# Linear attention: half of the next batch's scores move ahead of the second half's values

## The chip, the cores and the metric

The kernel runs on one core of a Trainium2 chip. The metric is the device time of one execution in microseconds (us), the median over several runs. Engines: TensorE (PE, its weight loads apart as PEld), VectorE (DVE), ScalarE (ACT), GpSimd (POOL) and SyncE (SP, which only starts transfers here).

## The reference, cut to what matters

The program is six layers over x of shape (8, 512, 128), each added to x: a mixture of experts, linear attention, the same experts again, a gated MLP with 4-bit rounding, softmax attention, and the MLP again. The change is in the linear attention:

```
qkv = (x @ qkv_w.T)                      # x normalised; 16 heads of 8
phi_q = relu(q) + EPS ; phi_k = relu(k) + EPS
kv = einsum('bhnd,bhne->bhnde', phi_k, v)
S = cumsum(kv, axis=2)                   # over the tokens n
out = einsum('bhnd,bhnde->bhne', phi_q, S)
out = out / max(scale * pos, EPS)
x = x + out @ proj_w.T
```

## The kernel before

All eight batches of x stay in SBUF. In this stage one body handles one batch i of 512 tokens, as 4 tiles of 128 tokens, each cut into 4 chunks of 32 tokens (c), and the 16 heads as 4 groups of 4 heads (g). The causal sum is split in two parts that add up in PSUM:

- within a chunk: `scores` multiplies keys by queries of the same 32 tokens, by head; VectorE masks them with the causal triangle (`scores` in its block, line 962) into `probs`; `within` multiplies the values by them.
- across chunks: `states` makes the key-value product of each chunk, ScalarE copies it out (`take_states`, line 547), GpSimd sums them up along the tokens (`linatt_prefix`, line 355), and `across` multiplies the summed states by the queries, onto the banks of `within`.

`within` and `across` are done in two halves, chunks 0 and 1, then chunks 2 and 3. Both halves use PSUM banks 6 and 7, so between them VectorE must take the result out. That is `pick`, the choice of heads: of four columns sets it keeps in each row the one of its own head, in three steps into `picked` (each counted on the semaphore `pick_part`), and a last one, in two parts, into `attT` (counted on `attT_ready`). The scores of one batch take 32 matmuls for each pair of groups; the pair 0 goes to banks 2 and 3, the pair 1 to banks 4 and 5. The matmuls appear as two records each in the trace.

The order on TensorE in body(i) is written by hand and looks ahead by one batch: input projection of batch i+1 (keys to bank 1, queries to bank 0, values to bank 2), turning of the keys (bank 3), `within` half 0 of batch i, `states` of i+1 (banks 2 to 5), `across` half 0, output projection of batch i-1 (bank 1), transposes of batch i+2 (bank 0), `within` half 1, `across` half 1, and all `scores` of batch i+1. The input projection waits until the output projection's result in bank 1 has been added to x (`residual`), which it knows from a signal of VectorE's later work: it waits for `attT_ready` of the whole `pick` of half 1.

VectorE in body(i): four masks of batch i, the keys of i+1 between the second and third, queries of i+1, statistics of a later batch, `pick` half 0, `residual` of batch i-1, `pick` half 1. ScalarE: queries, values and keys of batch i+1 out of PSUM, four copies of the queries with all heads but one zeroed (`q_bd`, line 539), four copies of the states, and the normalised rows of a later batch. Body 0, a loop of two passes with two bodies each (1 to 4), and bodies 5, 6 and 7 make up the stage. Body 7 has no next batch; its VectorE also begins the rounding of weights for a later layer.

Each engine runs its own list in order, and semaphores hold them together; `pe.wait_ge(s[...], n)` holds everything behind it on TensorE.

Of the kernel before, what the change touches and what calls it, by code (L numbers as in the profile page):

```python
# [24 lines left out]
P = 128  # L25
B, T, C = 8, 512, 128
TPB = T // P
# [4 lines left out]
CH = 32  # L32
NCH = P // CH
HQ = CH // HD
# [41 lines left out]
def macaron(nc, x, qkv_w, proj_w, alpha_log, beta_log, router_w, w1, w2,  # L76
            in_w, in_b, out_w, out_b, w_gate, w_up, w_down, out):
    with ExitStack() as ctx:
# [651 lines left out]
        def _(dve):  # L730
# [213 lines left out]
            def linatt(s, nxt):  # L944
                ch = Chain(dve, s["dve_chain"])

                def keys(i):

                    dve.wait_ge(s["k_done"], i + 1)
                    nc.vector.tensor_scalar(phi_k[:, :], bank(1, T), 0.0, ATT_EPS, ALU.max, ALU.add).then_inc(s["phik_ready"], 1)  # L950

                def queries(i):

                    dve.wait_ge(s["reluq_ready"], i + 1)
                    if type(i) is int and i == 0:
                        prep.settle()
                    nc.vector.scalar_tensor_tensor(phi_q[:, :], relu_q, ATT_EPS, pos[:, :],
                                                   ALU.add, ALU.mult).then_inc(s["phiq_ready"], 1)

                def scores(i, g, side):  # L960
                    dve.wait_ge(s["score_done"], 2 * i + g // 2 + 1)
                    nc.vector.tensor_tensor(probs[:, side, g, :, :, :].rearrange("p j h n -> p (j h) n"),
                                            bank(2 + g, TPB * HQ, CH),
                                            causal[:, :].unsqueeze(1).to_broadcast([P, TPB * HQ, CH]),
                                            ALU.mult).then_inc(s["probs_ready"], 1)

                def pick(i, half, side):

                    dve.wait_ge(s["att_done"], 2 * i + half + 1)
                    both = ps[:, 6:8, :].rearrange("p c (j h n) -> p (c j) h n", j=TPB, h=HQ)  # L970
                    nc.vector.tensor_scalar(picked[:, :, :], both[:, :, 0, :], headsel[:, 0:1], None,
                                            ALU.mult).then_inc(s["pick_part"], 1)
                    for hh in range(1, HQ - 1):

                        dve.wait_ge(s["pick_part"], 6 * i + 3 * half + hh)
                        nc.vector.scalar_tensor_tensor(picked[:, :, :], both[:, :, hh, :], headsel[:, hh:hh + 1],  # L976
                                                       picked[:, :, :], ALU.mult, ALU.add).then_inc(s["pick_part"], 1)

                    dve.wait_ge(s["pick_part"], 6 * i + 3 * half + 3)
                    for a in range(2):  # L980
                        c = 2 * half + a
                        t = nc.vector.scalar_tensor_tensor(attT[:, side, :, CH * c:CH * c + CH],
                                                           bank(6 + a, TPB, HQ * CH)[:, :, CH * (HQ - 1):CH * HQ],
                                                           headsel[:, HQ - 1:HQ], picked[:, TPB * a:TPB * a + TPB, :],
                                                           ALU.mult, ALU.add)
                    t.then_inc(s["attT_ready"], 1)

                def residual(i):
                    dve.wait_ge(s["proj_done"], i + 1)
                    nc.vector.tensor_tensor(group_b(i), bank(1, TPB, C), group_b(i), ALU.add).then_inc(s["x_done"], 1)  # L990

                def body(i, side):
                    more = known_below(i, GROUPS - 1)
                    scores(i, 0, side)
                    scores(i, 1, side)
                    if more:
                        keys(i + 1)
                    scores(i, 2, side)
                    scores(i, 3, side)
                    if more:  # L1000
                        queries(i + 1)
                    if known_below(i, GROUPS - 3):
                        ch.start(i * PER["linatt"] + pre)

                        dve.wait_ge(s["xn_ready"], i + 3)
                        ln_stats(s, ch, i + 3, TPB, tile_b)
                        assert ch.k == PER["linatt"], ("linatt", ch.k)
                    elif i == GROUPS - 3:
                        ch.start(i * PER["linatt"] + pre)
                        dve.wait_ge(s["xn_ready"], GROUPS)  # L1010
                        ln_stats(nxt, ch, 0, TPB, tile_b)
                    if not more:

                        dve.wait_ge(s_fw, 80)
                        w4.largest()
                        w4.scales()
                        w4.inverse()
                    pick(i, 0, side)
                    if not (type(i) is int and i == 0):
                        residual(i - 1)  # L1020
                    if not more:
                        w4.divide()
                    pick(i, 1, side)

                keys(0)
                queries(0)
                dve.wait_ge(s["xn_ready"], 2)
                ln_stats(s, ch, 2, TPB, tile_b)
                pre = ch.k
                linatt_bodies(dve, body)  # L1030
                dve.wait_ge(nxt["xn_ready"], 1)
                ln_stats(nxt, ch, 1, TPB, tile_b)
                residual(GROUPS - 1)
                dve.wait_ge(s["x_done"], GROUPS)
# [186 lines left out]
        def _(pe):  # L1221
# [98 lines left out]
            def linatt(s, nxt):  # L1320
                def project_in(i):
                    pe.wait_ge(s["xnT_ready"], i + 1)
                    if type(i) is not int or i > 1:

                        pe.wait_ge(s["attT_ready"], 2 * (i - 1))
                    mm(bank(1, T), wqkvT[:, 1, :], xnT[:, 0:T]).then_inc(s["k_done"], 1)
                    mm(bank(0, T), wqkvT[:, 0, :], xnT[:, 0:T]).then_inc(s["q_done"], 1)
                    if type(i) is not int or i > 0:

                        pe.wait_ge(s["probs_ready"], HQ * (i - 1) + 1)  # L1330
                    for j in range(TPB):
                        t = mm(bank(2, TPB, C)[:, j, :], tok(j), wqkvT[:, 2, :])
                    t.then_inc(s["v_done"], 1)
# [22 lines left out]
                                   tile_position=(CH * c, 0))  # L1356
                    t.then_inc(s["state_done"], 1)

                def scores(i, side):

                    pe.wait_ge(s["qbd_ready"], HQ * i + HQ)

                    pe.wait_ge(s["state_taken"], HQ * i + HQ)
                    pe.sem_inc(s_passed_pe, 1)
                    for pair in range(HQ // 2):
                        for j in range(TPB):
                            for c in range(NCH):
                                cols = slice(P * j + CH * c, P * j + CH * c + CH)
                                for g in (2 * pair, 2 * pair + 1):
                                    r = slice(CH * g, CH * g + CH)  # L1370
                                    t = mm(bank(2 + g, TPB, P)[CH * c:CH * c + CH, j, :], phi_k[r, cols],
                                           q_bd[r, side, :, cols], tile_position=(CH * g, CH * c))
                        t.then_inc(s["score_done"], 1)

                def within(i, half, side):

# [41 lines left out]
                def body(i, side):  # L1418
                    more = known_below(i, GROUPS - 1)
                    if more:  # L1420
                        project_in(i + 1)
                        turn_keys(i + 1)
                    within(i, 0, side)
                    if more:
                        states(i + 1, 1 - side)
                    across(i, 0, side)
                    if not (type(i) is int and i == 0):
                        project_out(i - 1, 1 - side, more)
                    if more:

                        pe.wait_ge(s["reluq_ready"], i + 2)
                        if known_below(i, GROUPS - 2):
                            transposes(s, i + 2)
                        else:
                            transposes(nxt, 0)
                    within(i, 1, side)
                    across(i, 1, side)
                    if more:
                        scores(i + 1, 1 - side)

                pe.wait_ge(s_wT, 2)
                project_in(0)
# [1 line left out]
                states(0, 0)  # L1444
                pe.wait_ge(s["reluq_ready"], 1)
                transposes(s, 1)
                scores(0, 0)
                linatt_bodies(pe, body)
                project_out(GROUPS - 1, 1, False)

# [200 lines left out]
```

## Time and profile before

| | |
|---|---|
| median of 3 runs | 820.65 us (819.05 to 822.27) |
| profiled execution | 819.17 us, its span 817.5 us |
| TensorE busy | 682.5 us, 83% of the span; mean granted clock 0.932 |
| VectorE, ScalarE, GpSimd busy | 77%, 58%, 29% |
| DMA | 7.00 MB, mean 9 GB/s |

The span runs from the first to the last instruction. The granted clock is TensorE's, as a share of full speed (2.4 GHz). Times in timelines are us from the start of the span. A few per cent of matmul records can be missing.

### The profile page before, as it was taken

To read this page: it belongs to the slowest core of one execution; us is meant where nothing else is said; L and a number is where in the kernel's file an instruction comes from. 1 tells how busy PE (TensorE), PEld (TensorE's weight loads), DVE (VectorE), ACT (ScalarE), POOL (GpSimd) and SP (SyncE) were. 2 spreads that over 40 slices of the span, in tenths; PEclk is the share of its full clock that TensorE was granted. 3 is DMA by queue.
4 is the path that set the end of the run, shared out by engine and by line. 5 is a ranking of instruction groups with operands and counts; after the bars stand their busy time and mean duration, and the time that the engine had idled before them with its cause. 6 is when DMAs were issued, how large, how long until landed. Compare 5 with 4: busy or idle time off the path is not lost.

```text
span 817.5 us, 16964 instructions
## 1 busy us (share of the span) xinstructions
PE 682.5 (83%) x5826; PEld 492.9 (60%) x5826; DVE 632.0 (77%) x1594; ACT 473.4 (58%) x915; POOL 239.5 (29%) x375
## 2 busy tenths in 40 slices
PE   5999999789988799999957788838898873787885
PEld 3777767577777667777734465534645652455654
DVE  2887888456655668878969999846999975899993
ACT  3877786664663078777755566526454214575652
POOL 5011020456455000110013543011643442345400
PEclk9999999699999699999978999978999995899997
DMA  8000000000000000000000000000000000000000
GB/s 210 2 0 0 0 1 1 2 3 4 0 1 4 2 1 0 0 0 1 0 1 0 1 0 0 0 0 2 1 0 0 0 1 0 1 26 13 23 16 26
DMA packets 13454, 7.00 MB, mean 9 GB/s; under 512 B 1176, under 2 KB 13408, under 8 KB 13408
## 3 DMA queue, kind: packets, MB, share of 16 engines
q1 hardware_dynamic: 11328, 5.33, 2.5%
q10 hardware_dynamic: 2080, 1.05, 0.5%
q8 instruction: 29, 0.48, 0.2%
q14 instruction: 17, 0.14, 0.1%
HBM read 4.28 MB, written 2.10 MB: 8 GB/s over the span
## 4 chain that ended last, share of the span: by engine, by line
PE 45%; DVE 36%; issue 10%; ACT 5%; POOL 2%; DVEq 1%; DMA 0%; ACTq 0%; POOLq 0%
PE ps L1250 41%; DVE ffn_work L786 4%; DVE shared L1046 3%; DVE shared L1074 3%; DVE x_sb L888 3%; DVE fq_h_max L753 2%; DVE ffn_work L1162 2%; DVE ffn_work L791 2%; DVE hq L797 2%; DVE picked L976 2%; DVE stats L822 2%; PE ps L1572 2%; ACT ffn_work L440 2%; ACT xn L470 2%; DVE ffn_work L780 1%
## 5 line engine op out<-in xcount | busy, mean ns | idle before, releaser
L1250 PEld LDWEIGHTS ps<-w_sb,sq_h 128*128 128x128 f32 x1024 | 131.4, 191 | 70.2 <-ACT sq_h L492 51.7
L888 DVE SCALAR_TENSOR_TENSOR x_sb<-ps,gates,x_sb 128x128 f32 (+1 forms) x512 | 147.1, 343 | 22.5 <-PE ps L1250 18.7
L1250 PE MATMUL ps<-w_sb,sq_h 128*128 128x128 f32 x1024 | 137.7, 277 | 1.5 <-ACT sq_h L492 1.4
L1250 PE MATMUL ps<-xnT,w_sb 128*128 128x512 f32 x256 | 135.2, 612 | 0.0
L310 POOL TENSOR_SCALAR vareps<-meanvar 128x4 f32<-128x4 f32 (+1 forms) x44 | 22.5, 511 | 354.3 <-DVE meanvar L831 338.3
L488 ACT ACTIVATE relu_h<-ps 128x512 f32<-128x512 f32 x128 | 75.7, 592 | 59.5 <-PE ps L1250 59.2
L470 ACT ACTIVATE xn<-x_sb,shift,rstd 128x128 f32 (+1 forms) x192 | 79.7, 481 | 17.6 <-POOL shift L318 17.6
L492 ACT ACTIVATE sq_h<-relu_h 128x512 f32<-128x512 f32 x128 | 80.6, 630 | 4.1
L676 ACT ACTIVATE hqT<-ps 128x384 f32<-128x384 f32 x64 | 30.0, 489 | 67.4 <-PE ps L1572 66.5
L1250 PE MATMUL ps<-gateT,xnT 128*128 128x352 f32 x128 | 56.8, 528 | 14.2 <-ACT ffn_work L670 10.7
L1250 PE MATMUL ps<-downT,hqT 128*128 128x128 f32 x384 | 62.7, 306 | 3.2 <-ACT hqT L676 3.0
L1572 PE MATMUL ps<-ident,hq 128*128 128x128 f32 x192 | 35.2, 313 | 34.9 <-DVE hq L797 34.9
L1250 PEld LDWEIGHTS ps<-downT,hqT 128*128 128x128 f32 x384 | 54.9, 215 | 9.3 <-ACT hqT L676 8.9
L355 POOL TENSOR_TENSOR shared<-shared 128x128 f32<-128x128 f32 x112 | 50.9, 455 | 28.9 <-ACT shared L547 20.8
L822 DVE BATCH_NORM_STATS2 stats<-x_sb 128x6 f32 (+1 forms) x192 | 40.7, 276 | 23.2 <-ACT xn L470 7.9
L1572 PEld LDWEIGHTS ps<-ident,hq 128*128 128x128 f32 x192 | 26.0, 161 | 48.0 <-DVE hq L797 48.0
L363 POOL TENSOR_TENSOR shared<-shared 128x512 f32<-128x512 f32 x32 | 42.8, 1365 | 39.3 <-DVE shared L1074 39.3
L440 ACT ACTIVATE ffn_work<-ffn_work 128x512 f32<-128x512 f32 (+2 forms) x33 | 33.5, 1015 | 34.2 <-DVE ffn_work L780 34.2
L1250 PE MATMUL ps<-upT,xnT 128*128 128x352 f32 x128 | 52.9, 498 | 0.0
L315 POOL TENSOR_TENSOR rstd<-vareps,minus_half 128x4 f32<-128x4 f32 (+1 forms) x44 | 51.3, 1166 | 3.7
L786 DVE SCALAR_TENSOR_TENSOR ffn_work<-ffn_work 128x512 f32<-128x512 f32 (+2 forms) x33 | 38.4, 1162 | 12.3 <-ACT ffn_work L440 12.2
L1046 DVE TENSOR_TENSOR shared<-shared 128x1024 f32<-128x1024 f32 x32 | 41.0, 1349 | 5.8 <-ACT shared L588 5.8
(156 smaller groups left out, 1265.5 us busy)
## 6 DMA issues: line engine op xcount, KB each, us to landing
x_sb<-in_L_attn_x_dram SPq DMA_DIRECT2D x8, 256.0 KB, 6.9
out_dram<-x_sb SPq DMA_DIRECT2D x8, 256.0 KB, 2.3
w_sb<-in_L_ffn_w_all_dram ACTq DMA_DIRECT2D x2, 512.0 KB, 6.1
wraw<-in_L_attn_qkv_w_dram SPq DMA_DIRECT2D x1, 192.0 KB, 4.9
wraw<-attn_in_proj_weight_dram SPq DMA_DIRECT2D x1, 192.0 KB, 4.1
fraw<-in_L_ffn_w_down_dram SPq DMA_DIRECT2D x1, 176.0 KB, 2.8
fraw<-in_L_ffn_w_gate_dram SPq DMA_DIRECT2D x1, 128.0 KB, 2.8
fraw<-in_L_ffn_w_up_dram SPq DMA_DIRECT2D x1, 128.0 KB, 2.5
```

Of the source, the lines that this page charges most:

```text
L315: nc.gpsimd.tensor_tensor(rstd[:, 0:n], vareps[:, 0:n], minus_half[:, 0:n], ALU.pow).then_inc(s["pool_chain"], 1)
L355: nc.gpsimd.tensor_tensor(st[:, k, :], st[:, k, :], st[:, k - 1, :], ALU.add).then_inc(s["prefix_ready"], 1)
L440: return nc.scalar.activation(m, v, ACT.Abs, scale=2.0 ** 22)
L470: a = nc.scalar.activation(xn[:, into + j, :], tile(i, j), ACT.Identity, scale=rstd[:, j:j + 1], bias=shift[:, j:j + 1])
L488: nc.scalar.activation(relu_h[:, e % 2, :], bank(2 + e % 2, T), ACT.Relu).then_inc(s["relu_done"], 1)
L492: nc.scalar.activation(sq_h[:, e % 2, :], relu_h[:, e % 2, :], ACT.Square).then_inc(s["sq_ready"], 1)
L786: self.t = self.ch.add(nc.vector.scalar_tensor_tensor(self.v, self.m, MAGIC, self.v, ALU.max, ALU.add))
L822: ch.add(nc.vector.bn_stats(stats[:, j, :], tile(i, j)))
L888: t = nc.vector.scalar_tensor_tensor(tile_b(i, j), bank(4 + e % 4, TPB, C)[:, j, :], gates[:, j, e:e + 1], tile_b(i, j), ALU.mult, ALU.add)
L1046: nc.vector.tensor_tensor(prod[:, b, :, :], kT[:, :, :], qT[:, b, :].unsqueeze(1).to_broadcast([P, B, P]), ALU.mult).then_inc(s["qk_ready" ...
L1250: return nc.tensor.matmul(o, a, b, start=start, stop=stop, **kw)
L1572: t = nc.tensor.transpose(bank(5 + j % 2, 3, P)[:, k, :], hq[:, j, P * k:P * k + P], ident[:, :])
```

## The change

Nothing is computed otherwise. On TensorE, `scores` does one pair of groups per call. Pair 0 of batch i+1 is issued after the transposes and before `within` half 1 of batch i, behind the waits for the queries by head and the taken states; pair 1 stays at the end of the body. On VectorE, the masks of groups 0 and 1 of batch i+1 are made in body i, between `residual` and `pick` half 1, and those of groups 2 and 3 in body i+1, behind the keys. The input projection waits for the first step of the second `pick` of the body before, no longer for the whole of it.

```
--- before.py
+++ after.py
@@ VectorE: body
                 def body(i, side):
                     more = known_below(i, GROUPS - 1)
-                    scores(i, 0, side)
-                    scores(i, 1, side)
                     if more:
                         keys(i + 1)
                     scores(i, 2, side)
...
                     pick(i, 0, side)
                     if not (type(i) is int and i == 0):
                         residual(i - 1)
+                    if more:
+                        scores(i + 1, 0, 1 - side)
+                        scores(i + 1, 1, 1 - side)
                     if not more:
                         w4.divide()
                     pick(i, 1, side)
...
                 ln_stats(s, ch, 2, TPB, tile_b)
+                scores(0, 0, 0)
+                scores(0, 1, 0)
@@ TensorE: project_in
                     if type(i) is not int or i > 1:
-                        pe.wait_ge(s["attT_ready"], 2 * (i - 1))
+                        pe.wait_ge(s["pick_part"], 6 * (i - 2) + 4)
@@ TensorE: scores
-                def scores(i, side):
-                    pe.wait_ge(s["qbd_ready"], HQ * i + HQ)
-                    pe.wait_ge(s["state_taken"], HQ * i + HQ)
-                    pe.sem_inc(s_passed_pe, 1)
-                    for pair in range(HQ // 2):
-                        for j in range(TPB):
...
-                        t.then_inc(s["score_done"], 1)
+                def scores(i, side, pair):
+                    if pair == 0:
+                        pe.wait_ge(s["qbd_ready"], HQ * i + HQ)
+                        pe.wait_ge(s["state_taken"], HQ * i + HQ)
+                        pe.sem_inc(s_passed_pe, 1)
+                    for j in range(TPB):
...
+                    t.then_inc(s["score_done"], 1)
@@ TensorE: body
                             transposes(nxt, 0)
+                        scores(i + 1, 1 - side, 0)
                     within(i, 1, side)
                     across(i, 1, side)
                     if more:
-                        scores(i + 1, 1 - side)
+                        scores(i + 1, 1 - side, 1)
...
-                scores(0, 0)
+                scores(0, 0, 0)
+                scores(0, 0, 1)
```

## Rows read from the trace of the kernel before

**Rows 1.** Windows, the stage: us, busy (records) of PE PEld DVE ACT POOL, clock, DMA
```profile
149.00:282.10 133.10, 114.75 (x2753) 95.67 (x2749) 78.37 (x200) 65.37 (x122) 63.90 (x143) 0.92 0.01 2
```

**Rows 2.** Timeline, PE, body 3: start, duration, what, [idle before <- releaser]
```profile
203.64 1.98 PE L1250 MATMUL ps<-xnT,wT 128*128 128x512 f32 x4 [0.30 <-DVE attT L982]
...
206.88 1.15 PE L1250 MATMUL ps<-shared,v_tok 32*32 32x128 f32 x64
...
209.07 1.83 PE L1250 MATMUL ps<-shared 128*128 128x128 f32 x14
...
211.63 0.60 PE L1258 MATMUL ps<-ident,xn 128*128 128x128 f32 x4
213.25 1.14 PE L1250 MATMUL ps<-shared,v_tok 32*32 32x128 f32 x64 [1.02 <-DVE attT L982]
...
216.31 2.03 PE L1250 MATMUL ps<-shared,phi_k 32*32 32x128 f32 x128
218.64 1.98 PE L1250 MATMUL ps<-xnT,wT 128*128 128x512 f32 x4 [0.31 <-DVE attT L982]
```

**Rows 3.** Timeline, DVE, the same body and the next one's start
```profile
212.50 0.61 DVE L982 SCALAR_TENSOR_TENSOR attT<-ps,headsel,picked 128x128 f32<-128x128 f32 x2
...
216.42 0.48 DVE L971 TENSOR_SCALAR picked<-ps,headsel 128x256 f32<-128x256 f32 x1 [2.71 <-PE ps L1250]
...
218.50 1.28 DVE L962 TENSOR_TENSOR shared<-ps,causal 128x512 f32<-128x512 f32 x2
219.80 0.69 DVE L950 TENSOR_SCALAR phi_k<-ps 128x512 f32<-128x512 f32 x1
220.41 1.28 DVE L962 TENSOR_TENSOR shared<-ps,causal 128x512 f32<-128x512 f32 x2
```

**Rows 4.** Timeline, ACT, the same body
```profile
205.66 0.60 ACT L532 ACTIVATE ffn_work<-ps 128x512 f32<-128x512 f32 x1 [6.12 <-PE ps L1250]
...
209.97 2.41 ACT L547 ACTIVATE shared<-ps 32x512 f32<-32x512 f32 x4
```

**Rows 5.** Timeline, POOL, the same body
```profile
212.46 7.39 POOL L355 TENSOR_TENSOR shared<-shared 128x128 f32<-128x128 f32 x14 [1.86 <-ACT shared L547]
```

**Rows 6.** Timeline, PE: body 0's second values, first and last waiting projection
```profile
168.18 1.23 PE L1250 MATMUL ps<-shared,v_tok 32*32 32x128 f32 x64 [1.92 <-DVE attT L982]
...
173.65 1.98 PE L1250 MATMUL ps<-xnT,wT 128*128 128x512 f32 x4 [0.31 <-DVE attT L982]
...
248.79 1.95 PE L1250 MATMUL ps<-xnT,wT 128*128 128x512 f32 x4 [0.40 <-DVE attT L982]
```

**Rows 7.** Timelines of PE, DVE and ACT, end of body 6 and body 7
```profile
258.47 1.32 PE L1250 MATMUL ps<-shared,v_tok 32*32 32x128 f32 x64 [1.02 <-DVE attT L982]
...
266.52 1.96 PE L1250 MATMUL ps<-shared,v_tok 32*32 32x128 f32 x64 [2.79 <-DVE shared L962]
268.41 3.35 PE L1250 MATMUL ps<-shared 128*128 128x128 f32 x14
...
263.90 2.48 DVE L962 TENSOR_TENSOR shared<-ps,causal 128x512 f32<-128x512 f32 x4
...
255.09 2.41 ACT L547 ACTIVATE shared<-ps 32x512 f32<-32x512 f32 x4
```

**Rows 8.** Timeline, PEld: body 3, and (156.84) the projection behind body 0's scores
```profile
213.22 0.90 PEld L1250 LDWEIGHTS ps<-shared,v_tok 32*32 32x32 f32 x64 [1.23 <-issue]
214.32 1.86 PEld L1250 LDWEIGHTS ps<-shared 128*128 128x128 f32 x16 [0.20 <-issue]
216.31 1.76 PEld L1250 LDWEIGHTS ps<-shared,phi_k 32*32 32x32 f32 x128
...
156.84 0.50 PEld L1250 LDWEIGHTS ps<-xnT,wT 128*128 128x128 f32 x2 [0.38 <-issue]
```

**Rows 9.** Windows around the hole before body 7, columns as in rows 1
```profile
265.00:266.50 1.50, 0.00 (x0) 0.01 (x1) 1.50 (x4) 0.00 (x0) 0.04 (x1) 0.89 0.00 0
266.50:268.00 1.50, 1.48 (x57) 1.50 (x64) 1.44 (x3) 0.00 (x0) 0.00 (x0) 0.50 0.00 0
```

More of the change, by code:

```diff
@@ L1357, in states @@
                     t.then_inc(s["state_done"], 1)
-                def scores(i, side):
-                    pe.wait_ge(s["qbd_ready"], HQ * i + HQ)
-                    pe.wait_ge(s["state_taken"], HQ * i + HQ)
-                    pe.sem_inc(s_passed_pe, 1)
-                    for pair in range(HQ // 2):
-                        for j in range(TPB):
[L1367 to L1372, printed above, removed]
-                        t.then_inc(s["score_done"], 1)
+                def scores(i, side, pair):
[4 more added lines that the diff above has]
+                    for j in range(TPB):
+                        for c in range(NCH):
+                            cols = slice(P * j + CH * c, P * j + CH * c + CH)
+                            for g in (2 * pair, 2 * pair + 1):
+                                r = slice(CH * g, CH * g + CH)
+                                t = mm(bank(2 + g, TPB, P)[CH * c:CH * c + CH, j, :], phi_k[r, cols],
+                                       q_bd[r, side, :, cols], tile_position=(CH * g, CH * c))
+                    t.then_inc(s["score_done"], 1)
                 def within(i, half, side):
```

## The prediction

> **What bounds the kernel now.** I read the page first. The stage of the change is one of six that run one after the other, and it takes about 133 of the 817.5 us at a mean granted clock of 0.92 [rows 1]. The next stage's first TensorE instruction waits until this stage's last residual is added, so time saved here can't be hidden by another stage. Then I read the timeline of the stage, engine by engine, over one batch in the steady part.
>
> One body takes 15.00 us, from one input projection to the next (203.64 to 218.64) [rows 2]. In it TensorE stands still twice. Ahead of the second half's values it waits 1.02 us for VectorE's choice of heads, which the chain of waits puts on the path that sets the end. Ahead of the projection it waits 0.31 us for the second choice. All else is TensorE work end to end. VectorE idles 2.71 us before the second choice [rows 3], ScalarE 6.12 us before it takes the queries [rows 4], GpSimd 1.86 us before its prefix sums [rows 5]. So TensorE with the two choices is the ring that sets the pace, and only work taken out of the two holes, or put in them, counts.
>
> The pattern holds for bodies 1 to 6: the first of these six projections begins at 173.65, the last at 248.79, the one with a wait of 0.31, the other of 0.40 [rows 6]. Body 7 has no next batch: there TensorE stands for 2.79 us while VectorE makes the choice and then four masks, 2.48 us of them [rows 7].
>
> **The change part by part.** No instruction is added or removed; 64 of the 128 score records of each next batch move, two of the four masks move, and one wait is loosened. No DMA is touched.
>
> *First half of the scores into the hole.* They need the queries by head and the taken states of that batch, the last of which ScalarE ends at 209.97 + 2.41 = 212.38 [rows 4]. TensorE is through with its transposes at 211.63 + 0.60 = 212.23 [rows 2]. I allow 0.10 us from the signal to the first matmul (VectorE's choice ends at 212.50 + 0.61 = 213.11, the weight load it releases begins at 213.22 [rows 3, 8]); so the half begins at 212.48. Whole, the scores take 2.03 us [rows 2]; half is 1.02, so it ends at 213.50. Behind it in TensorE's queue stands the second half's values, which could begin at 213.25 before: they lose 0.25 us.
>
> *Second half of the scores.* From the values' start to the scores' start are 216.31 - 213.25 = 3.06 us [rows 2], unchanged; the second half begins at 216.56. Its weight loads take half of 1.76, to 217.44 [rows 8].
>
> *What the projection then waits for.* The new wait asks only for the first step of the second choice. VectorE begins the choice 0.03 us after the matmuls end, so at 216.42 + 0.25 = 216.67, and its first step takes 0.48 [rows 3]: 217.15, earlier than TensorE gets there. But the projection's weight load now stands directly behind the scores. No row shows this at full clock without a wait. Bounds: 0.20 us of idle on the load queue, where a full-width load follows 32-wide ones at full clock, and 0.38, the very same transition at half clock in body 0 [rows 8]. I take 0.25, nearer to the first because the clock is full here. The projection begins at 217.44 + 0.25 = 217.69, against 218.64: **0.95 us a body**, with ends of 1.00 and 0.82.
>
> The Trainium skill (TensorE: Matmul & The Clock Gate, "Part 3: Packing small matmuls") says that a weight load overlaps matmuls in flight only when it targets other rows of the array. This speaks against the change, since the projection's load takes all rows and the scores fill the lower ones to the last. By its figure for one load of 128 columns (0.11 us, an estimate from that page) the exposed time would be smaller than the 0.25 that I take, and the saving 1.09 a body.
>
> *Both parts lean on each other.* Were only the scores moved, the projection would still wait for the whole second choice, which begins 0.25 later: 218.64 + 0.25, a loss. The loosened wait is what turns the filled hole into time.
>
> *Does VectorE keep up?* Its next instruction after the choice is now the keys, not the masks. The choice takes 218.50 - 216.42 = 2.08 us to the next start [rows 3], so keys can start at 218.75, 1.06 after the projection's start, where they started 1.16 after it before. The keys' projection is ready then, give or take 0.1 us: it is the first two of four records of 1.98 us together [rows 2]. The masks 2 and 3 start 220.41 - 219.80 = 0.61 after the keys and last 1.28 [rows 3], so they end at 220.64. The first half's values wait for them; TensorE comes to those 206.88 - 203.64 = 3.24 us after the projection's start [rows 2], at 220.93. So the masks are hidden with about 0.2 us to spare; every tenth beyond that would be paid. Masks 0 and 1 now run in VectorE's idle time between the residual, which ended at 216.42 - 2.71 = 213.71, and the second choice (216.67) [rows 3]. The first half of the scores is done by then, two masks last 1.28, and 1.7 us are left. Without that cover they would cost 1.28 a body.
>
> *ScalarE and GpSimd.* ScalarE's work for a body hangs on the projection, so its last state copy stays 8.74 us behind the projection's start. GpSimd's prefix sums end at 212.46 + 7.39 = 219.85 [rows 5]; the first half's prefix matmuls of the next body ran 5.43 us after the projection (209.07 [rows 2]), which is 223.1 in the new time. Spare 3.3 us. Hidden, nothing.
>
> *Body 7.* In body 6 the states are taken at 255.09 + 2.41 = 257.50, so the values begin at about 258.62, not 258.47: 0.15 later [rows 7]. After the choice only two masks stand, not four: 2.48 - 1.28 = 1.20 us less. Body 7's values begin 1.05 us earlier relative to body 6.
>
> **Sum.** Six projections (bodies 1 to 6) x 0.95 = 5.70, and 1.05 at body 7: 6.75 us. The profiled execution took 819.17 us (its span is 817.5, 1.7 lie around it), so it would become 812.4; the median of the runs is 820.65, 1.5 above the profiled one, and gives **813.9**. The cost of splitting a stream in two is bounded below by nothing and above by 64 records at 1.14 (the values) instead of 1.02 [rows 2]: 0.12 twice a body, 1.4 in all, which makes 815.3. I take nothing, since part of the 1.14 is the drain that overlaps the next matmuls.
>
> **Rivals.**
>
> *The clock stays up in body 7.* After the hole of 2.79 us the granted clock is 0.50 from 266.5 on, and it fell in the last part of the hole (mean 0.89 from 265.0 to 266.5) [rows 9], so half speed (1.2 of 2.4 GHz). Values and prefix matmuls take 1.96 + 3.35 = 5.31 us there, where the same at full clock take 1.15 + 1.83 = 2.98 [rows 2, 7]. The hole becomes about 2.6 us (scores end a microsecond earlier, values begin 1.05 earlier). It is barely shorter; after body 0's hole of 1.92 the values took 1.23 us [rows 6], so the clock was up. If it stays up here, 2.3 us more are won: 811.6. The Trainium skill (TensorE: Matmul & The Clock Gate, "Part 1: The HAM clock gate") says that idleness throttles and activity releases, which allows it; the trace agrees in direction (0.50 after the hole), not on how near the edge this is. Chance 0.13.
>
> *ScalarE becomes the bound, lightly.* With the scores ahead of the values, the state copies now sit on the ring: projection, queries, copies by head, four state copies, scores, values. Each 0.1 us by which they come later is paid in seven bodies. Half a microsecond late leaves 6.75 - 7 x 0.5 = 3.25 us: 817.4, no measurable change. For it: the slack that ScalarE had (212.38 against the 213.22 of the values) is gone. Against it: it idles 6.12 us before each body's work, and its copies repeat to the hundredth. Chance 0.09.
>
> *The same, heavily: slower.* It decides from 1.0 us on (6.75 / 7), and is measurable on the slow side from 1.6 us: 6.75 - 11.2 = -4.4, 825.1. The place is the wait for the taken states in front of the first half of the scores. What would have to happen is that copies out of the four PSUM banks, or the copies by head, slow from 0.6 to some 0.8 us each. Nothing in the rows does this. Chance 0.03.
>
> *VectorE's masks take over* in front of the first half's values, where they have 0.2 us to spare: if they come 0.5 us later than worked out, 0.3 a body is lost, and 6 x 0.65 + 1.05 = 4.95 us remain: 815.7. Still faster. Chance 0.12. The forecast itself has 0.63.
>
> **Numbers.** Likeliest 813.9. The three runs of before lie within 3.2 us, so no less than 0.5% (4.1 us) can be told from no change. The range takes in the clock rival on its low side and the two light ones on its high side, without the slow one: 810.8 to 817.2. Faster by over 0.5%: forecast, clock and masks, 0.63 + 0.13 + 0.12, less a little for the spread of the runs, 0.86; the same 0.11; slower 0.03.
>
> **What would show it.** Right: bodies of about 14.05 us; no idle TensorE time before the projection that VectorE releases; before the scores' first half about 0.25 us released by ScalarE's state copies; the values right behind it without a wait; in body 7 two masks before them. Wrong: a body over 14.4 us, with the idle before the first half's values (released by masks) or before the scores (released by state copies) grown; or a granted clock under 1.00 in bodies 1 to 6, where each microsecond of matmuls would cost two.

## The result, and the profile after

| | before | changed |
|---|---|---|
| median | 820.95 us (12 runs) | 813.76 us (12 runs) |
| lowest to highest | 819.05 to 822.42 | 809.42 to 818.32 |
| profiled execution | 819.17, span 817.5 | 818.32, span 816.5 |

The ratio is 0.9923 with a 95% interval of 0.9897 to 0.9949: faster by 0.8%, the 813.9 of the forecast within 0.2 us. But the runs of the changed kernel lie over 8.9 us, those of before over 3.4, and the profiled execution is the slowest of the twelve. A second trace of the same kernel (below) comes from a run of 811.38 us. The spread goes with TensorE's mean granted clock: of these twelve runs and six more made later, the ten of 809.4 to 814.3 us show 0.930 to 0.937, the eight of 816.3 to 818.3 us show 0.925 to 0.928. So the median lies between two groups, and where the difference comes from is found below only in part.

The stage, timed from body 0's scores to the next stage's first router matmul, went from 128.71 us to 123.62. Its steady part is as forecast. The timeline of TensorE in the changed kernel, body 4 (the line numbers have moved by three):

```profile
216.88 1.98 PE L1253 MATMUL ps<-xnT,wT 128*128 128x512 f32 x4
...
224.90 0.60 PE L1261 MATMUL ps<-ident,xn 128*128 128x128 f32 x4
225.72 1.14 PE L1253 MATMUL ps<-shared,phi_k 32*32 32x128 f32 x64 [0.21 <-issue]
226.65 1.14 PE L1253 MATMUL ps<-shared,v_tok 32*32 32x128 f32 x64
227.73 2.05 PE L1253 MATMUL ps<-shared 128*128 128x128 f32 x16
229.71 1.15 PE L1253 MATMUL ps<-shared,phi_k 32*32 32x128 f32 x64
230.79 1.98 PE L1253 MATMUL ps<-xnT,wT 128*128 128x512 f32 x4
```

Against [rows 2]: the body takes 13.91 us, not 15.00. The two waits of 1.02 and 0.31 are gone. In the first stands the first half of the scores, 0.21 us behind the transposes, and the projection follows the second half at once. On ScalarE and VectorE, the same body:

```profile
223.21 2.41 ACT L547 ACTIVATE shared<-ps 32x512 f32<-32x512 f32 x4
```

```profile
226.92 1.29 DVE L962 TENSOR_TENSOR shared<-ps,causal 128x512 f32<-128x512 f32 x2
229.82 0.48 DVE L971 TENSOR_SCALAR picked<-ps,headsel 128x256 f32<-128x256 f32 x1 [1.61 <-PE ps L1253]
...
231.96 0.69 DVE L950 TENSOR_SCALAR phi_k<-ps 128x512 f32<-128x512 f32 x1
232.56 1.28 DVE L962 TENSOR_TENSOR shared<-ps,causal 128x512 f32<-128x512 f32 x2
```

The last state copy ends at 223.21 + 2.41 = 225.62, and the scores begin at 225.72: the 0.21 of "issue" is ScalarE. Masks 0 and 1 lie in the old idle time, which [rows 3] had at 2.71 us and which is 1.61 now; keys start 1.17 us after the projection, as they did.

Not as forecast are bodies 0 and 6 (and body 2, for which see the points below). Here the second half's prefix matmuls are torn in two:

```profile
170.03 1.14 PE L1253 MATMUL ps<-shared,v_tok 32*32 32x128 f32 x59
171.10 1.27 PE L1253 MATMUL ps<-shared 128*128 128x128 f32 x9
172.92 0.94 PE L1253 MATMUL ps<-shared 128*128 128x128 f32 x7 [0.55 <-issue]
...
255.67 1.05 PE L1253 MATMUL ps<-shared 128*128 128x128 f32 x7
257.48 1.27 PE L1253 MATMUL ps<-shared 128*128 128x128 f32 x9 [0.76 <-issue]
...
262.29 1.96 PE L1253 MATMUL ps<-shared,v_tok 32*32 32x128 f32 x64 [2.46 <-DVE shared L962]
264.18 3.35 PE L1253 MATMUL ps<-shared 128*128 128x128 f32 x14
```

Between records of one stream, with no semaphore between them, stand gaps of 0.55 and 0.76 us. The DMA view for 254 to 258 us has one transfer, and no data queue in it:

```profile
GB/s 0 0 0 0 0 0 0 0 0 0 164 0 0 0 0 0 0 0 0 0 0 0 0 0 0 0 0 0 0 0 0 0 0 0 0 0 0 0 0 0
DMA packets 1, 0.02 MB, mean 4 GB/s; under 512 B 0, under 2 KB 0, under 8 KB 0
...
q8 instruction: 1, 0.02, 1.5%
```

It is an instruction transfer at 255.0 us, 2.5 us before the stream goes on. The view for 168 to 172 us shows the same at 170.3, 2.6 us before 172.92. For 204 to 234 us, where the loop's second pass runs, it shows no packet at all, and no gap is there:

```profile
DMA packets 0, 0.00 MB, mean 0 GB/s; under 512 B 0, under 2 KB 0, under 8 KB 0
```

Body by body, each from one projection's start to the next (body 6 to body 7's values, body 7 to the router), in us:

| | 0 | 1 | 2 | 3 | 4 | 5 | 6 | 7 |
|---|---|---|---|---|---|---|---|---|
| before | 16.81 | 15.00 | 14.99 | 15.00 | 15.09 | 15.06 | 17.73 | 15.58 |
| changed | 16.93 | 13.92 | 14.17 | 13.91 | 13.91 | 13.85 | 17.65 | 15.84 |

### The profile page after: what moved, and what is told of

It is laid out like the page before. It is cut to its first block, busy times and chain, and to the rows that moved or that the text cites. A ratio compares the mean times of both kernels' runs of the same rounds, so it can differ in the third digit from the quotient of the medians.

```text
span 816.5 us, 16970 instructions
## 1 busy us (share of the span) xinstructions
PE 687.0 (84%) x5826; PEld 497.9 (61%) x5826; DVE 632.5 (77%) x1594; ACT 473.4 (58%) x915; POOL 237.2 (29%) x375
## 3 DMA queue, kind: packets, MB, share of 16 engines
q1 hardware_dynamic: 11328, 5.33, 2.5%
q10 hardware_dynamic: 2080, 1.05, 0.5%
## 4 chain that ended last, share of the span: by engine, by line
PE 51%; DVE 31%; issue 10%; ACT 5%; POOL 2%; DVEq 1%; DMA 0%; ACTq 0%; POOLq 0%
PE ps L1253 47%; DVE ffn_work L786 4%; DVE shared L1049 3%; DVE shared L1077 3%; DVE fq_h_max L753 2%; DVE ffn_work L1165 2%; DVE ffn_work L791 2%; DVE hq L797 2%; PE ps L1577 2%; DVE stats L822 2%; ACT ffn_work L440 2%; ACT xn L470 2%; PE ps L1261 1%; DVE ffn_work L780 1%; DVE fq_h_r L772 1%
## 5 line engine op out<-in xcount | busy, mean ns | idle before, releaser
L1253 PE MATMUL ps<-downT,hqT 128*128 128x128 f32 x384 | 64.6, 313 | 3.0 <-ACT hqT L676 2.8
L1253 PEld LDWEIGHTS ps<-downT,hqT 128*128 128x128 f32 x384 | 56.7, 222 | 9.1 <-ACT hqT L676 8.8
```

What stands on the lines that cost most here:

```text
L1253: return nc.tensor.matmul(o, a, b, start=start, stop=stop, **kw)
```

## The experiments

"Stage" is always the time from body 0's scores to the next router matmul in the run's one trace; a ratio is to the runs of the kernel before that were made with it, with its 95% interval.

### Each part alone

```
# wait only, in project_in of the kernel before
-  pe.wait_ge(s["attT_ready"], 2 * (i - 1))
+  pe.wait_ge(s["pick_part"], 6 * (i - 2) + 4)
# move only: the changed kernel with that line as it was
```

> Only the projection's wait is loosened, the scores and masks stay as they were. Theory (the parts lean on each other): the projection begins about 0.3 us earlier in each body, but VectorE's keys still stand behind the choice and two masks and the first half's values behind four masks, so a body goes from 15.00 to no less than 14.8 us; the stage gains 0 to 1.5 us and the kernel is within 0.2% of before. Rival (each part brings its own share): the whole 0.31 us wait goes in six bodies, 1.9 us.

> The scores and masks are moved, the projection waits for the whole second choice as before. Theory: the projection waits about 1.0 us in each body and the body takes 15.0 to 15.25 us, so six bodies lose up to 1.5 us and body 7 gains about 1; the kernel is at 820 to 822 us, no faster than before. Rival (each part brings its own share): a body takes about 14.2 us and the kernel gains 5 us.

| | ratio | bodies 1 to 5 |
|---|---|---|
| wait only | 0.9990 (0.9975 to 1.0004) | 14.67 to 15.23 us |
| move only | 1.0012 (0.9996 to 1.0029) | 15.17 to 15.27 us |

TensorE in a body with the wait alone, and in one with the move alone:

```profile
219.65 1.98 PE L1250 MATMUL ps<-xnT,wT 128*128 128x512 f32 x4
...
223.21 1.14 PE L1250 MATMUL ps<-shared,v_tok 32*32 32x128 f32 x64 [0.25 <-DVE shared L962]
...
229.57 1.14 PE L1250 MATMUL ps<-shared,v_tok 32*32 32x128 f32 x64 [1.03 <-DVE attT L982]
```

```profile
204.56 1.98 PE L1253 MATMUL ps<-xnT,wT 128*128 128x512 f32 x4 [1.18 <-DVE attT L982]
...
213.41 1.14 PE L1253 MATMUL ps<-shared,phi_k 32*32 32x128 f32 x64 [0.27 <-issue]
```

Loosened alone, the wait comes back 3.6 us later, in front of the first half's values, released by the four masks. Moved alone, the scores fill the hole of 1.02 us and the projection waits 1.18 instead of 0.31. Each half is worth nothing, both together 0.8%. The rival that each brings its own share fell in both. The wait alone was expected to take 0 to 1.5 us off the stage and to leave no body under 14.8; body 3 took 14.67, and the stage of its trace (of the slowest of its twelve runs, 824.99 us) was 130.48, 1.8 longer than before, since the clock fell in body 6, which took 19.63 us. The move alone has the two gaps of the changed kernel, of 0.55 and 0.66 us.

### ScalarE, before and after

```
                     front(i + 1, 1 - side)
+                    nc.scalar.activation(extra[:, :, :], w1_sb[:, 0:4, :], ACT.Copy)
                     take_states(i + 1, 1 - side)
```

> The changed kernel with one more copy of 128x512 from SBUF to SBUF on ScalarE ahead of each body's state copies (its result is used by nothing), some 0.5 to 0.6 us in bodies 0 to 6. Theory (ScalarE's state copies now sit on the ring, with no slack): each body grows by the full 0.5 to 0.6, to 14.4 or 14.5 us, the idle time before the scores' first half from 0.22 to about 0.8; the stage grows by 3.5 to 4 us. Rival (TensorE or VectorE alone sets the pace): bodies stay at 13.9.

> The kernel before with the same additional copy on ScalarE as in the run of the changed kernel. There the state copies end 0.8 us before TensorE needs anything of them, and the next use is the transposed rows and the prefix sums. Theory (in the kernel before ScalarE is off the ring): bodies stay at 15.0 us, the kernel within 0.2% of before. Rival (ScalarE's length counted already): bodies at 15.3 to 15.6, the kernel 2 to 4 us slower.

The additional copy takes 0.62 us, with 0.52 to the next start. In the changed kernel the bodies 1 to 5 take 14.37 to 14.68 us, and TensorE waits 0.73 where it waited 0.21:

```profile
224.12 0.62 ACT L564 ACTIVATE extra<-w_sb 128x512 f32<-128x512 f32 x1
224.64 2.41 ACT L548 ACTIVATE shared<-ps 32x512 f32<-32x512 f32 x4
```

In the kernel before they stay at 14.99 to 15.08, with the waits of 0.31 and 1.02 as they were. Ratios: 0.9956 (0.9942 to 0.9970) and 0.9998 (0.9985 to 1.0012). The stage of the changed kernel with the copy took 127.61 us, 4.0 and 7.0 more than in the two traces without it, where 3.5 to 4 was expected: in bodies 0 and 6 the clock fell as well. So the place that the forecast gave to the ScalarE rivals is real: the ring now runs through the state copies, 0.52 us on ScalarE is 0.52 us a body, and it had been free. The cause that these rivals needed, slower copies, did not occur.

### The changed kernel again

> The changed kernel once more, for a second trace and more times. Its first trace shows two gaps in TensorE's stream that before had not: 0.55 us in body 0 and 0.76 in body 6, both inside the second half's prefix matmuls, released by nothing, with a 16 KB instruction transfer just ahead. Theory (instruction supply): the gaps stand at the same two places again, within 0.3 us of the same size, since the code lies at the same place. Rival (chance, or the clock): at least one is gone or elsewhere. Time 809 to 818 us as in the first runs, ratio 0.99.

Median 815.21 us of 6 runs, ratio 0.9929 (0.9904 to 0.9954). The gaps are at the same places, smaller: 0.28 and 0.49 us against 0.55 and 0.76. The stage took 120.61 us.

```profile
170.46 0.94 PE L1253 MATMUL ps<-shared 128*128 128x128 f32 x7 [0.28 <-issue]
...
255.04 1.27 PE L1253 MATMUL ps<-shared 128*128 128x128 f32 x9 [0.49 <-issue]
```

### Moving the code

```
         def _(pe):
+            for _k in range(N):               # N = 96; 30; 30 here and 50 in later waits
+                pe.sem_inc(s_passed_pe, 1)
             pe.wait_ge(s_ident, 1)
```

> The changed kernel with 96 semaphore signals more at the very start of TensorE's program, where it waits for the input anyway. Nothing else moves but the place of all later TensorE code, by 6 KB where instruction transfers bring 16 KB each. Theory (instruction supply): the two gaps of 0.55 and 0.76 us move to other matmuls, grow, shrink or go; bodies 0 and 6 change by 0.3 us or more each, the loop's bodies stay at 13.9. Rival (the gaps belong to these matmuls): both stay where they are, sizes within 0.1.

> The changed kernel with 30 semaphore signals at the start of TensorE's program, where it idles 5.3 us for the router's weights: the later code lies about 2 KB further on. In the run with 96 signals the first matmul came at 15.67 us (before: 5.33), so one signal costs at most about 0.16 us and 30 should cost nothing. Theory (instruction supply): the stage from body 0's scores to the next stage's router changes by 1 us or more against 120.6 to 123.6, with gaps at other matmuls than body 0's and body 6's prefix matmuls. Rival (gaps belong to those matmuls, and the run with 96 lost its time otherwise): 120.6 to 123.6 us, gaps where they were.

> The changed kernel with 80 signals, 30 at the start, 20 before the first transposes (3.9 us idle there) and 12, 9 and 9 in the three waits ahead of body 0 (2.2, 1.7 and 1.6 us idle): the stage's code lies 5 KB further on. Theory: near the run with 96 (6 KB), a gap of 1 to 2 us inside body 1's values or just after, a lower clock behind it, and a stage of 126 to 129 us. Rival: 120.6 to 123.6 us.

> The kernel before with the same 80 signals. Its bodies hold 1.3 us of waits each, in which the supply of instructions can catch up. Theory (the waits that the change took away had covered the supply): the stage stays within 1 us of its 128.7 and the kernel within 0.3% of before. Rival (any placement can hurt either kernel): a gap released by nothing appears here too and the stage takes 130 us or more.

| kernel, signals added | ratio | stage | gaps between records (us, what is left of the stream behind them) |
|---|---|---|---|
| changed, 0 | 0.9923 | 123.62; 120.61 | body 0: 0.55; 0.28, 7 of 16 prefix records; body 6: 0.76; 0.49, 9 of 16 |
| changed, 30 | 0.9996 (0.9981 to 1.0011) | 129.37 | body 0: 1.64, 6 of 64 values; body 6: 1.59, 8 of 64 |
| changed, 80 | 0.9951 (0.9927 to 0.9975) | 127.16 | body 1: 1.39, 2 of 64 values |
| changed, 96 | 1.0071 (1.0036 to 1.0106) | 128.85 | body 1: 1.69, 10 of 64 values; body 6: 1.22 and 0.99 |
| before, 80 | 1.0006 (0.9995 to 1.0017) | 132.56 | body 6: 1.56, 4 of 32 state records |

Thirty instructions, executed in a wait (TensorE's first matmul comes at 5.61 us, before at 5.33), take the whole gain away. With 96 the start itself suffers: the first matmul comes at 15.67 us, the first transposes at 17.73 instead of 9.49, 8.2 us of the loss. The rest is in the stage. TensorE with 30 signals, in body 0:

```profile
168.38 1.09 PE L1255 MATMUL ps<-shared,v_tok 32*32 32x128 f32 x56
171.10 0.64 PE L1255 MATMUL ps<-shared,v_tok 32*32 32x128 f32 x6 [1.64 <-issue]
171.67 3.78 PE L1255 MATMUL ps<-shared 128*128 128x128 f32 x16
175.38 1.96 PE L1255 MATMUL ps<-shared,phi_k 32*32 32x128 f32 x64
177.27 3.75 PE L1255 MATMUL ps<-xnT,wT 128*128 128x512 f32 x4
```

and with 96, in body 1:

```profile
190.17 1.07 PE L1255 MATMUL ps<-shared,v_tok 32*32 32x128 f32 x54
192.93 0.66 PE L1255 MATMUL ps<-shared,v_tok 32*32 32x128 f32 x10 [1.69 <-issue]
193.51 3.78 PE L1255 MATMUL ps<-shared 128*128 128x128 f32 x16
```

Two things are to be seen. First, the gap moves by as many instructions as were put in. A record goes with one weight load, so it stands for two instructions. From 0 to 30 the gap of body 0 moves from 7 prefix records left to 16 and 6 of the values: 15 records, 30 instructions. That of body 6 moves from 9 to 16 + 8, 15 records again; and from 80 to 96 that of body 1 from 2 to 10, which is 8 records, 16 instructions. With 96 there are two gaps in body 6, before the last 13 records of the states and the last 41 of the second half's values: 126 records lie between them, 252 instructions, with the waits and signals on top. A gap belongs to a place in the code, not to a matmul. Second, more is lost than the gap itself: behind it the prefix matmuls take 3.78 us instead of 2.05, the scores 1.96 instead of 1.15, the projection 3.75 instead of 1.98, and the granted clock of this stretch is at its lower level:

```profile
171.00:177.00 6.00, 5.90 (x86) 5.18 (x85) 1.44 (x3) 0.00 (x0) 3.31 (x8) 0.50 0.01 3
```

That the gap pulls the clock down is possible, not shown: it fell behind the gaps of 1.39, 1.59, 1.64 and 1.69 us, but stayed up behind those of 0.18 to 1.22 us and behind the one of 1.56 in the kernel before, and in three traces it fell in a body without a gap (wait alone, body 6; the longer ScalarE, bodies 0 and 6; the kernel before with 80 signals, body 1: prefix matmuls of 3.39 to 3.82 us). Body 0 takes 20.27 us, 3.3 more than in the changed kernel's trace.

For the kernel before I was half wrong. Its total is untouched by 80 signals, but it isn't immune: a gap of 1.56 us stands in the state matmuls ahead of body 6's half, and the stage of its trace, 132.56 us, is where the rival had it (130 or more; the trace is from the slowest of its twelve runs). The other half of the 3.9 us by which that stage is longer has no gap: in body 1, of 16.99 us, the second half's values come 0.35 us later and the clock falls behind them.

### Placing the code by count

The same shift, made cheaply with small matmuls at TensorE's start:

```
             pe.wait_ge(s_ident, 1)
+            for _k in range(44):              # 64 in the other
+                nc.tensor.matmul(bank(7, CH)[0:CH, :], ident[0:CH, 0:CH], ident[0:CH, 0:CH], ...)
             pe.wait_ge(s_r, 16)
```

> The changed kernel with 44 small matmuls (32x32 of the identity into a PSUM bank that nothing uses yet) at TensorE's start, where it idles until 5.3 us; each is two weight loads and two matmul records, so the later code lies 176 instructions (11 KB) further on. Counting back from where the gaps stood with 0, 30, 80 and 96 more instructions, each body's code has one critical boundary of 256 instructions, 58 instructions earlier in the next body; with 176 none of those of bodies 0, 1, 2, 5 and 6 falls at the end of the dense stretch of scores and values. Theory (placement): no gap over 0.3 us released by nothing in bodies 1 to 6, the stage at 118 to 121 us, the kernel at 810 to 813 us, at least as fast as the changed kernel and with less spread. Rival (the count is wrong or gaps come from elsewhere): a gap of 0.5 us or more in body 1, 5 or 6, the stage at 123 us or more.

> The same with 64 small matmuls, 256 instructions, exactly one piece of 16 KB. Theory (placement counts by the place within a piece): the gaps are back where the changed kernel has them, inside the second half's prefix matmuls of bodies 0 and 6, 7 and 9 records before their end (within 2), 0.3 to 0.8 us, and the time is the changed kernel's, 811 to 816 us. Rival (the matmuls at the start, which warm the clock or add code, act by themselves): as the run with 44.

> The kernel before with the 44 small matmuls. It tells what they do by themselves and what this placement does to the kernel before, whose trace shows no gap released by nothing in bodies 1 to 6. Theory: within 0.3% of before (818.5 to 822.5). Rival (the start's matmuls save time by themselves): 2 us or more faster.

| | ratio | runs | stage | bodies 0, 6, 7 |
|---|---|---|---|---|
| changed, 176 | 0.9925 (0.9909 to 0.9941) | 813.51 to 816.38 (6) | 119.76 | 15.78, 16.39, 14.17 |
| changed, 256 | 0.9931 (0.9904 to 0.9958) | 810.96 to 818.94 (7) | 119.42 | 16.09, 17.53, 12.58 |
| before, 176 | 0.9994 (0.9982 to 1.0006) | 818.08 to 821.49 (12) | 128.80 | 16.63, 17.45, 15.72 |

With 176 no stream is torn, and body 6 takes 16.39 us, as it does with 80 signals, where it has no gap either. The second half's prefix matmuls in body 6, and what follows:

```profile
253.85 2.05 PE L1255 MATMUL ps<-shared 128*128 128x128 f32 x16
255.83 1.15 PE L1255 MATMUL ps<-shared,phi_k 32*32 32x128 f32 x64
259.45 1.38 PE L1255 MATMUL ps<-shared,v_tok 32*32 32x128 f32 x64 [2.46 <-DVE shared L962]
```

With 256, TensorE in body 6:

```profile
254.86 1.05 PE L1255 MATMUL ps<-shared 128*128 128x128 f32 x7
256.66 1.16 PE L1255 MATMUL ps<-shared 128*128 128x128 f32 x9 [0.76 <-issue]
...
261.37 1.14 PE L1255 MATMUL ps<-shared,v_tok 32*32 32x128 f32 x64 [2.46 <-DVE shared L962]
262.44 1.83 PE L1255 MATMUL ps<-shared 128*128 128x128 f32 x14
```

The gap is back, before the same 9 records and of the same 0.76 us; in body 0 it stands before 6 records (0.18 us) where it stood before 7. So for these gaps the place within a piece of 256 instructions counts. The 44 small matmuls do nothing by themselves, as the kernel before shows.

But the placement without gaps brought no faster kernel: 814.24 us at the median, where 810 to 813 was expected, with the stage's 119.76 within its forecast. In that trace the rest of the program took 538.28 us, 2.8 more than with 256 instructions (535.45), which hides what the stage won. Its runs lie closer together, over 2.9 us, though six runs are few. No version here beats the changed kernel clearly.

## Why the prediction was right, point by point

**The hole filled, 0.95 us a body.** Measured 1.08 to 1.21 in bodies 1 and 3 to 5 (13.85 to 13.92 against 15.00 to 15.09). The terms: state copies end 8.73 to 8.74 us after the projection's start (forecast 8.74), 0.10 to the scores (0.10), 0.93 to 0.94 to the values (1.02), 3.05 to 3.06 to the second half (3.06), 1.08 to 1.09 to the projection (0.88 + 0.25 = 1.13). The terms that were off are the half of the scores, 0.08 too long because 2.03 us holds a drain that the next matmuls cover, and the exposed weight load: between the last of the scores' weight loads and the projection's the load queue idles 0.20 us, the lower bound. The weight loads of body 3's end:

```profile
215.79 0.88 PEld L1253 LDWEIGHTS ps<-shared,phi_k 32*32 32x32 f32 x64
216.87 0.30 PEld L1253 LDWEIGHTS ps<-xnT,wT 128*128 128x128 f32 x2 [0.20 <-issue]
```

The Trainium skill (TensorE: Matmul & The Clock Gate, Part 3) says that a weight load overlaps matmuls in flight only when it targets other rows; this row agrees, with 0.20 us of idle before a load that takes all rows, above the 0.11 that its figure gave. Body 2 takes 14.17, and 14.15 to 14.36 in the five others (again, and 30, 96, 176 and 256 instructions on) where nothing else disturbs it: it is the one at whose end the loop goes back. Its extra time stands before the next projection:

```profile
202.97 1.98 PE L1253 MATMUL ps<-xnT,wT 128*128 128x512 f32 x4 [0.18 <-DVE picked L976]
```

The profile puts this wait down to the second step of VectorE's choice, though the loosened wait asks only for the first, which had ended at 201.74 + 0.48 = 202.22; in the second trace the same 0.18 us is "issue". That the jump costs the 0.3 us, hidden before by the wait of 0.30, is argued and not shown. The forecast, which took all six bodies as alike, had nothing for it.

**Both parts lean on each other.** Shown by the two halves alone. The move alone makes bodies of 15.17 to 15.27 us, where the forecast had 15.00 + 0.25.

**VectorE keeps up with 0.2 us to spare, ScalarE joins the ring.** Right: no wait for masks is seen, and a longer ScalarE is paid in full. The spare time was about 0.1 us less than worked out, since the keys start 1.15 to 1.17 us after the projection and not 1.06.

**Body 7, 1.05 us.** Without a gap body 6 takes 16.39 against 17.73, 1.34 less. In the changed kernel's trace it takes 17.65, 1.26 more: the gap of 0.76, and 0.5 by which the stream runs slower just ahead of it and behind it. This is the step that the prediction lacked. It counted the instructions that move, but not the time in which they have to be brought.

**The clock rival** (0.13) was laid out rightly and happens, but not by this change alone. The hole before body 7 is 2.46 us in both traces above; in the changed kernel's the values behind it take 1.96 us, in the one with 256 instructions 1.14, and body 7 is 15.84 against 12.58. Windows over body 7, the changed kernel and the one with 256 instructions:

```profile
262.29:278.13 15.84, 11.79 (x174) 10.56 (x175) 9.87 (x25) 1.16 (x1) 1.38 (x3) 0.72 0.01 2
```

```profile
261.37:273.95 12.58, 8.08 (x174) 7.14 (x175) 9.87 (x25) 1.16 (x1) 0.47 (x3) 0.99 0.01 3
```

The gain is 3.3 us, more than the 2.3 that I gave it: 2.35 of it lie ahead of the second half, as forecast, and 0.92 in the last output projection and what follows, which I had left out (it takes 2.07 us in the one and 1.16 in the other). It is more common than the 0.13: over body 7 the mean clock is 0.72 in all five traces of the kernel before and its variants, whose hole is 2.53 to 2.79 us, but 0.76 to 0.99 in six of the nine of the changed kernel and its variants. Since the same kernel shows 0.72 in one trace and 0.81 in the other, the change makes it possible at most; that the shorter hole is the cause is likely and not shown.

**The sum.** Forecast -6.75 us. For the stage the two traces of the changed kernel show -5.09 and -8.10, the one without gaps -8.95, the one with 256 instructions -9.29, all against one trace of before. In us:

| against before | up to body 6 | body 7 | clock over body 7 (before 0.72) |
|---|---|---|---|
| changed | -5.35 | +0.26 | 0.72 |
| again | -6.41 | -1.69 | 0.81 |
| 176 | -7.54 | -1.41 | 0.88 |
| 256 | -6.29 | -3.00 | 0.99 |

The whole kernel: -7.2 between the medians. That this meets the forecast within 0.2 us of the time is in part luck. The bodies brought some 0.8 us more than I gave them (6.20 for bodies 0 to 5 and 1.34 for body 6 in the run without gaps), and the gaps, 0.77 us together in one trace and 1.31 in the other, took that or more away. The clock does the rest: in body 7 as in the table, and in body 0, where 0.93 of the 1.11 us between the two traces of the changed kernel lie ahead of the scores (mean clock 0.79 and 0.87 there). The sum had neither the gaps nor the clock. The range was also said to take in the lighter ScalarE rival, whose 817.4 lies just above its end of 817.2.

**What stays open.** The rest of the program, from the router to the end, took 534.6 to 536.0 us in nine of the fourteen traces and 538.3 to 538.6 in the other five. Both kinds of kernel are in both groups (before 535.4; wait alone 538.4; changed 538.4 and 535.9). So 3 us of the spread are no doing of the change, and the first trace of the changed kernel had bad luck there as well. The clock differs there too: 260 to 280 us behind the router's first matmul it is 0.66 in the first trace of the changed kernel and 0.80 in the second. What sets it was not tried. Neither was why the placement without gaps has no better median, beyond the slow rest in its one trace.

## What to carry to other kernels

Look for the ring before moving work into a hole: here the hole's work only paid once the wait at the other end was loosened, and each of the two edits alone measured as nothing. A filled hole also takes cover away: the engine that had slack (ScalarE), and the supply of instructions. A change of a per cent in a kernel with thousands of small matmuls should be measured with a few dozen harmless instructions put in front of it as well, or a lucky or unlucky placement is taken for the edit. Where runs of one kernel differ by more than the effect, compare their granted clocks before explaining the difference.

## What the runs showed of the hardware

TensorE's instructions arrive in transfers of 16 KB (256 of them). In code that runs for the first time, a stream of 32x32 matmuls uses 256 instructions in about 2 us (64 scores and 64 values records with their loads: 0.94 + 1.07). The instructions behind a boundary ran 2.3 to 2.6 us after their transfer began (four transfers: 170.3 and 255.0 above, 168.6 with 30 signals, 254.4 with 256 instructions). Where such a boundary fell towards the end of that stretch, just behind it, or in the states matmuls behind a half's values, TensorE stood for 0.2 to 1.7 us. The second pass of the loop (bodies 3 and 4) moved nothing and had no gap. The Trainium skill (Runtime: NRT & Kernel Launch, "Instruction fetch mechanics") gives blocks of 16 KiB, 256 instructions, and calls the crossing of a boundary mostly hidden; the size agrees with the return of the gap after 256 instructions, the hiding does not hold for these streams, which lost up to 1.7 us.
